# Row maxima and softmax sums that change layout by DMA, biases that leave TensorE or fill its rows, and a new order of the steps

## The reference

```python
B, S, D = 8, 512, 128
xn = layernorm(x)                                  # no affine part
out = x + attn(xn, W_qkv, W_out) + ffn(xn, ...)
# attn: 16 heads of 64, rotary embedding on q and k, causal softmax(q k / 8) v, times W_out
# ffn:  q, k, v = xn W + b; 16 heads of 8; full softmax(q k / sqrt(8)) v; a = that Wo + bo
#       x2 = xn + layernorm(a, g1, be1); gate = softmax(x2 Wg + bg); best 2 of 8 experts
#       m = sum over the 2 of gate * (x2 We[e] + bexp[e]);  ffn = x2 + layernorm(m, g2, be2)
```

## Time and profile before

| what | value |
|---|---|
| time, median of 3 runs | 1494.18 us (1490.78 to 1495.87) |
| the profiled execution | 1491.08 us, its span 1489.3 us |
| granted clock of PE, mean | 0.939 of full |
| PE busy | 1366.0 us, 92% |
| DVE, POOL, ACT busy | 920.0, 826.8, 797.6 us |
| HBM traffic | 5.59 MB read, 2.10 MB written |

### The profile page before, as it was taken

One profiled execution on the slowest core, in us unless ns is written; L12 is line 12 of the kernel. 1 busy time (PEld: TensorE's weight loads), 2 busy tenths in 40 slices (PEclk: granted clock), 3 DMA queues, 4 the chain that ended last, 5 costly groups with the idle time before them and its releaser, 6 DMA issues.

```text
span 1489.3 us, 27676 instructions
## 1 busy us (share of the span) xinstructions
PE 1366.0 (92%) x9896; PEld 842.6 (57%) x9896; DVE 920.0 (62%) x2324; ACT 797.6 (54%) x1103; POOL 826.8 (56%) x797
## 2 busy tenths in 40 slices
PE   0779999989999999989999899997999899999986
PEld 0455556646665566645576455654666555764544
DVE  5437547855567746775478655785458664786624
ACT  1256564566545664555644656454655566446550
POOL 0745557466656558355573666655564655826621
PEclk9779998999889998999989999899999999899997
DMA  3201111010101111011110111001010111101000
GB/s 108 50 8 24 28 33 33 22 36 23 29 23 29 32 28 36 8 36 30 29 30 22 36 30 29 23 22 36 23 39 13 36 30 29 30 17 34 23 1 7
DMA packets 37516, 43.04 MB, mean 29 GB/s; under 512 B 9342, under 2 KB 20870, under 8 KB 37256
## 3 DMA queue, kind: packets, MB, share of 16 engines
q1 hardware_dynamic: 34200, 38.33, 10.8%
q10 hardware_dynamic: 3184, 2.95, 0.7%
HBM read 5.59 MB, written 2.10 MB: 5 GB/s over the span
## 4 chain that ended last, share of the span: by engine, by line
PE 71%; POOL 9%; DMA 5%; ACT 4%; DVE 4%; issue 3%; SPq 2%; ACTq 0%; POOLq 0%; DVEq 0%
PE work L925 9%; PE work L833 8%; PE work L950 8%; PE work L834 5%; PE work L835 5%; PE work L837 5%; PE work L1008 4%; PE work L939 4%; PE work L971 4%; DMA swapped<-raw 3%; PE work L980 3%; PE work L901 3%; SPq L399 2%; PE work L997 2%; POOL raw L437 2%
## 5 line engine op out<-in xcount | busy, mean ns | idle before, releaser
L696 DVE TENSOR_REDUCE fnmax<-work 128x2 f32<-128x1024 f32 x256 | 301.4, 1218 | 102.8 <-PE work L980 102.5
L518 ACT ACTIVATE fpt<-work 128x1024 f32<-128x1024 f32 x256 | 250.1, 1024 | 117.3 <-PE work L997 116.1
L437 POOL TENSOR_TENSOR raw<-raw,cos_t 128x512 f32<-128x512 f32 x128 | 164.1, 1282 | 247.3 <-DMA swapped<-raw 246.6
L794 DVE CUSTOM_DVE_ANT_0 work<-work,causal 128x512 f32<-128x512 f32 (+3 forms) x512 | 235.5, 522 | 69.0 <-PE work L901 69.0
L454 POOL TENSOR_SCALAR_AFFINE_SELECT pt<-pt 128x256 f32<-128x256 f32 x128 | 49.7, 410 | 296.0 <-ACT pt L566 296.0
L566 ACT ACTIVATE pt<-work 128x1024 f32<-128x1024 f32 (+1 forms) x192 | 163.4, 882 | 93.4 <-PE work L925 89.1
L446 POOL TENSOR_TENSOR qk_l<-raw,qk_h 128x512 fp32r<-128x512 f32 x128 | 162.2, 1278 | 22.3 <-ACT qk_h L548 22.3
L441 POOL TENSOR_TENSOR raw<-raw,swapped 128x512 f32<-128x512 f32 x128 | 163.8, 1279 | 10.0
L438 POOL TENSOR_TENSOR swapped<-swapped,sin_t 128x512 f32<-128x512 f32 x128 | 164.1, 1282 | 0.0
L950 PE MATMUL work<-pt,v 128*64 128x512 f32 (+3 forms) x1024 | 158.3, 453 | 0.0
L1008 PE MATMUL work<-fpt,fv 128*9 128x512 f32 x1024 | 123.4, 593 | 0.8 <-DVE u L811 0.8
(11 more groups left out here) (167 smaller groups left out, 2688.5 us busy)
## 6 DMA issues: line engine op xcount, KB each, us to landing
swapped<-raw SPq DMA_DIRECT2D x512, 64.0 KB, 2.0
x_in<-in_L_attn_x_dram SPq DMA_DIRECT2D x8, 256.0 KB, 3.0
out_dram<-x_in SPq DMA_DIRECT2D x8, 256.0 KB, 2.3
fpt<-in_L_attn_W_qkv_dram ACTq DMA_DIRECT2D x1, 1536.0 KB, 6.8
pt<-in_L_ffn_We_dram ACTq DMA_DIRECT2D x1, 512.0 KB, 9.9
wout<-in_L_attn_W_out_dram ACTq DMA_DIRECT2D x1, 512.0 KB, 10.0
pt<-in_rope_dram ACTq DMA_DIRECT2D x1, 192.0 KB, 7.9
affine<-in_L_ffn_g_dram SPq DMA_DIRECT2D x2, 64.0 KB
```

Of the source, the lines that this page charges most:

```text
L437: nc.gpsimd.tensor_tensor(raw[:, n % 3], raw[:, n % 3], cos_t[:], ALU.mult)
L518: nc.scalar.activation(fpt[:, i, 2 * r:2 * r + 2].rearrange("p h n -> p (h n)"), bank_of(("fst", b, g, i), 2 * r, 2), ACT.Exp, scale=1.0 / ...
L696: nc.vector.tensor_reduce(fnmax[:, j, 2 * r:2 * r + 2, 0:1], bank_of(("fsm", b, g, j), 2 * r, 2).rearrange("p (f n) -> p f n", f=2), AX.X, ...
L794: ins = nc.vector.tensor_tensor_reduce(out=scores, in0=scores, in1=causal[:, S - n:S], scale=-1.0, scalar=3.0e38, op0=ALU.add, op1=ALU.min ...
```

## The change

It does five things.

1. **Row maxima.** `nmax` becomes 128 x 8 without gaps, and one transpose gives 8 rows of 128. `row` copies them to `m_rows`, and a new SP step `mrow` puts them by four DMAs of two rows into rows 0 and 64 of `max_row`, which is zero elsewhere. `st` waits for `mrow`. In the full attention `fnmax` becomes 128 x 16, `fsub` is a copy of 16 rows to `fm_rows`, and a new SP step `fput` writes them by four DMAs into rows 0, 32, 64, 96 of `fqk`; `fst` waits for it.
2. **Softmax sums.** `lT`, `fan`, `rT`, `rb` go. SP steps take their place: `lc` spreads each of four rows of `l_rows` over 128 partitions x 4, `inv` works on that, `lr` writes each inverse back as one row, `lw` copies each row to 64 partitions of `l_wide`. `lw` waits on SP until `lr` has landed; `div` waits for `lw`.
3. **Biases.** Those of `moe`, `fv`, `wo` become passes of 128 rows: `pick_row` (ones in rows 0 and 64) by `biases` (bias in row 0, its rest in row 64). Those of `fqk` go from PE: `fqkh` becomes two ACT operations with scale and bias, and `fqkl` adds a bias per partition. That of `gate` is added by DVE in `gsub`.
4. **Start.** 24 small DMAs load `qk_bias`, one `bg_rows`.
5. **Order.** All numbers of `START`, `PSUM` and `PERIOD` (170.28 to 158.1397) are new.

The core of the diff:

```diff
-    "mT": [16.58, 25.78, 57.5, 78.17, 108.69, 121.66, 144.89, 165.47],
+    "mT": [17.141, 61.043, 75.721, 95.372, 108.783, 128.409, 142.363, 154.925],
-PERIOD = 170.28
+PERIOD = 158.1397
-    "SP": ("swap", "store", "load"),
+    "SP": ("swap", "mrow", "lc", "lr", "lw", "fput", "store", "load"),
+PARTS = {"mrow": T, "lc": 4, "lr": 2, "lw": 2, "fput": T}
...
+                elif kind == "mrow":
+                    c = x_[2]
+                    sp.wait_ge(*after("row", b, c))
+                    sp.wait_ge(*after("st", *ring(1, b, c, NC), 2))
+                    for t in range(T):
+                        sp.dma_start(max_row[0:P:DH, t * P:(t + 1) * P].bitcast(F32), m_rows[2 * t:2 * t + 2].bitcast(F32)).then_inc(done["mrow"], 16)
+                elif kind == "lc":
+                    c = x_[2]
+                    sp.wait_ge(*after("lsb", b, c))
+                    sp.wait_ge(*after("inv", *ring(1, b, c, NC)))
+                    for n in range(4):
+                        row = l_rows[n * STRIP:n * STRIP + 1].rearrange("o (p j) -> o p j", j=T)
+                        sp.dma_start(l_part[:, n // 2, n % 2], row).then_inc(done["lc"], 16)
+                elif kind == "lr":
+                    c = x_[2]
+                    sp.wait_ge(*after("inv", b, c))
+                    sp.wait_ge(*after("lw", *ring(1, b, c, NC)))
+                    for h in range(2):
+                        row = r_rows[h:h + 1].rearrange("o (p j) -> o p j", j=T)
+                        sp.dma_start(row, l_inv[:, h]).then_inc(done["lr"], 16)
+                elif kind == "lw":
+                    c = x_[2]
+                    sp.wait_ge(*after("lr", b, c))
+                    sp.wait_ge(*after("div", *ring(1, b, c, NC)))
+                    for h in range(2):
+                        sp.dma_start(l_wide[h * DH:(h + 1) * DH], r_rows[h:h + 1].unsqueeze(1).broadcast_to([1, DH, S])).then_inc(done["lw"], 16)
+                elif kind == "fput":
+                    g = x_[2]
+                    sp.wait_ge(*after("fsub", b, g))
+                    for t in range(T):
+                        sp.dma_start(fqk[0:P:STRIP, g % 2, 0, t * P:(t + 1) * P].bitcast(F32), fm_rows[t * GH:(t + 1) * GH].bitcast(F32))\
+                            .then_inc(done["fput"], 16)
...
-                    nc.scalar.copy(fqk[:, g % 2].rearrange("p k n -> p (k n)"), bank_of(("fqk", b, g), 0, 2)).then_inc(done["fqkh"], 1)
+                    for k, low in enumerate((q_low, k_low)):
+                        ins = nc.scalar.activation(fqk[:, g % 2, k], bank_of(("fqk", b, g), k), ACT.Identity, scale=low,
+                                                   bias=qk_less[:, k, g:g + 1])
...
-                            out=fqk[:, g % 2, k], in0=fqk[:, g % 2, k].bitcast(F32), scalar=low, in1=bank_of(("fqk", b, g), k),
-                            op0=ALU.mult, op1=ALU.add)
+                            out=fqk[:, g % 2, k], in0=bank_of(("fqk", b, g), k), scalar=qk_bias[:, k, g:g + 1],
+                            in1=fqk[:, g % 2, k].bitcast(F32), op0=ALU.add, op1=ALU.add)
...
-                    nc.vector.tensor_tensor(fqk[:, g % 2, 0], bank_of(("fmT", b, g)), fqk[:, g % 2, 0].bitcast(F32),
-                                            ALU.add).then_inc(done["fsub"], 1)
+                    nc.vector.tensor_copy(fm_rows, bank_of(("fmT", b, g))[0:T * GH, 0:P]).then_inc(done["fsub"], 1)
...
-                                     (one_rows("bv"), bias_rows("bv")))
+                                     (pick_row[:], bias_of("bv")))
...
-                    for t in range(T):
-                        ins = nc.tensor.transpose(psum[:, tile(t)], nmax[:, t:t + P], ident)
-                    ins.then_inc(done["mT"], 1)
+                    nc.tensor.transpose(psum[0:2 * T, 0:P], nmax[:].rearrange("p t h -> p (t h)"), ident).then_inc(done["mT"], 1)
```

More of the change, by code:

```diff
@@ L51 @@
 START = {
[L52 to L67, removed]
@@ L96 @@
[L96 to L108, removed]
@@ new lines @@
+    "fT": [135.67, 161.633, 194.364, 220.297],
+    "fdiv": [143.344, 175.071, 192.304, 216.292],
+    "cT": [222.856],
+    "ch": [225.402],
+    "cl": [218.06],
+    "wo": [225.483],
+    "ln1": [224.091],
+    "rs1": [219.833],
+    "nm1": [235.204],
+    "x2": [251.609],
+    "x2T": [242.267],
+    "x2h": [257.623],
+    "x2l": [247.399],
+    "gate": [254.513],
+    "gsub": [260.49],
+    "gexp": [279.268],
+    "pick": [270.752],
+    "moe": [266.171, 267.623, 268.968, 272.316],
+    "moew": [278.221, 278.665, 278.678, 278.686],
@@ L145 @@
-    "fv": [3],
-    "fqk": [2, 1, 1, 1],
-    "fsm": [4, 2, 4, 4, 4, 0, 4, 4, 4, 4, 4, 0, 2, 4, 0, 4],
-    "fmT": [2, 0, 0, 6],
-    "fst": [2, 4, 4, 4, 4, 0, 2, 4, 4, 2, 4, 4, 4, 2, 4, 2],
-    "fpv": [3, 0, 0, 0],
-    "fT": [0, 0, 0, 0],
-    "cT": [0],
-    "wo": [2],
-    "x2T": [1],
-    "gate": [6],
-    "moe": [0, 2, 0, 2],
-    "proj": [6, 1, 6, 1, 7, 6, 0, 3, 2, 0, 5, 6, 0, 4, 0, 2],
[9 rows of a table removed]
+    "xT": [2],
+    "fv": [1],
+    "fqk": [4, 0, 6, 5],
+    "fsm": [2, 2, 4, 4, 4, 2, 0, 0, 3, 3, 4, 0, 4, 4, 4, 4],
@@ L167 @@
+    "fmT": [3, 0, 2, 2],
+    "fst": [0, 1, 3, 1, 1, 4, 0, 1, 2, 0, 2, 0, 3, 0, 0, 2],
+    "fpv": [5, 1, 7, 6],
+    "fT": [7, 3, 7, 3],
+    "cT": [2],
+    "wo": [0],
+    "x2T": [0],
+    "gate": [4],
+    "moe": [4, 2, 6, 0],
+    "proj": [6, 2, 0, 1, 2, 2, 4, 7, 2, 3, 0, 7, 0, 4, 2, 7],
[7 rows of a table added]
 }
-PERIOD = 170.28
+PERIOD = 158.1397
 ENGINE = {
     "PE": ("xT", "fv", "fqk", "fsm", "fmT", "fst", "fpv", "fT", "cT", "wo", "x2T", "gate", "moe", "proj", "v", "sm", "mT",
-           "st", "ls", "pv", "lT", "rT", "ao"),
-    "ACT": ("xh", "fvc", "fqkh", "fexp", "fo", "ch", "x2h", "gexp", "raw", "hi", "vc", "row", "exp", "lsb", "fan", "rb"),
+           "st", "ls", "pv", "ao"),
+    "ACT": ("xh", "fvc", "fqkh", "fexp", "fo", "ch", "x2h", "gexp", "raw", "hi", "vc", "row", "exp", "lsb"),
@@ L191 @@
         KEYS[kind] = [(c, unit, h) for c in range(NC) for unit in range(3) for h in range(2)]
-    elif kind in ("mT", "row", "tri", "ls", "lsb", "pv", "lT", "inv", "fan", "rT", "rb", "div"):
+    elif kind in ("mT", "row", "mrow", "tri", "ls", "lsb", "lc", "lT", "inv", "fan", "rT", "rb", "lr", "lw", "pv", "div"):
         KEYS[kind] = [(c,) for c in range(NC)]
@@ L556, in _ @@
                     act.wait_ge(*after("mT", b, c))
-                    act.wait_ge(*after("st", *ring(1, b, c, NC), 2))
-                    nc.scalar.copy(max_row[:], bank_of(("mT", b, c))).then_inc(done["row"], 1)
+                    act.wait_ge(*after("mrow", *ring(1, b, c, NC)))
+                    nc.scalar.copy(m_rows, bank_of(("mT", b, c))[0:2 * T, 0:P]).then_inc(done["row"], 1)
                 elif kind == "exp":
```

304 lines of the change are left out of this document (141 added, 163 removed), and 22 rows, old and new, of tables (PSUM, START).

## The result

The changed kernel takes **2094.63 us** (median of 4 runs, 2092.39 to 2100.75) beside 1492.48 us for the kernel before on the same chip (4 runs, 1480.22 to 1495.87). The ratio is 1.406, 95% interval 1.398 to 1.415: slower by 602 us, where 1405 us and a gain were forecast. The range, 1340 to 1465 us, does not hold it. The profiled execution took 2092.39 us, its span is 2090.7 us, and its granted clock was 0.80 after 0.939.

What follows compares the result with a forecast made beforehand. PE was taken to bound the kernel at 166.3 us per batch. Taking off 24.7 and giving back 14 saves 10.7 over seven batches; with -12 for fill and drain and +1 for start, 1491.1 becomes 1405 us, range 1340 to 1465.

Steps and rivals of the forecast that it cites:

- What bounds the kernel, and what PE loses: PE bounds the steady stage at 166.3 us per batch; fewer bias passes and transposes take 24.7 us per batch off it.
- A microsecond removed from PE is a microsecond gained, until waits take its place: In every batch, less PE work shortens the time one for one until waits replace it; PE alone would allow 141.6 us.
- Landing of `lw`: Copy of each inverse row to `l_wide`: a landing of 2.0 us, 2.6 us for the step with two issues.
- The chain of sums: Softmax sums to `div` through `lsb`, `lc`, `inv`, `lr`, `lw`: 10.2 us instead of about 3.4, costed at nothing on PE.
- Give-back of the row maxima: Waits before `st` and `fst` for `mrow` and `fput` give back 14 us per batch, bounds 5 and 22.
- Start: 25 more small DMA issues put the last load 7 us later; +1 us taken in all.
- Fill and drain: Both ends, bound by one batch's chain: less other PE work between steps but longer hops; -12 us, bounds 0 and -25.
- SP becomes the bound: Rival: small SBUF copies issue so slowly (1.3 us) that SP sets a 186 us period, 1630 us in all; chance 0.07.
- In-order DVE: Rival: `inv` and `div` wait for landings and hold up `fmax` and `max` behind them; 56 us more, 1461 us; chance 0.09.
- Clock: Rival: PE's granted clock falls around eight waits per batch, costing 50 us in all, 1455 us; chance 0.08.
- Bias passes keep their gap: Rival: full-height bias passes of `moe`, `wo`, `fv` gain nothing, 4.9 us per batch less, 1444 us; chance 0.03.
- too low: Signs that the give-back was underestimated: granted clock below 0.9, or DVE's waits for `l_part` and `l_wide` ending ahead of PE waits.

Runs made afterwards that it cites:

- e5: The changed kernel without `lr` and `lw`, `u` multiplied by a row of cosines, output not normalised: 1495.3 us, ratio 1.003 to the kernel before.
- g1: e5 with the row maxima as before the change (four transposes, no `mrow` or `fput`), output not normalised: 1420.76 us, ratio 0.954.
- f1: The kernel before, in its own order, with the change's biases alone: 1451.0 us, ratio 0.975.
- f6: f1 with `lc` taking the softmax sums from row to column by DMA in place of `lT`: 1457.1 us, ratio 0.981.
- e1: The changed kernel with each `lw` reading 64 partitions of a constant table instead of one row 64 times, output not normalised: 1645.22 us, ratio 1.104.
- e2: The changed kernel with `lw` copying an eighth of the columns, still from one partition, most output not normalised: 1645.84 us, ratio 1.104.
- e3: The changed kernel with `lw` kept, but `div` waiting for `inv` instead of it, output not normalised: 1789.95 us, ratio 1.201.
- g4: The changed kernel with `div` placed later in DVE's list in seven of eight head pairs: 2121.47 us, ratio 1.426.
- g6: e4 with `div` placed later in DVE's list, as in g4: 1715.22 us, ratio 1.153.
- f4: All mechanisms of the change, with the slow `lw`, in the order of the kernel before: 1910.66 us, ratio 1.284.
- g5: e1 with `div` placed later in DVE's list, as in g4, output not normalised: 1697.94 us, ratio 1.141.
- e4: The changed kernel with the inverses written to a DRAM row by `lr` and read from there by `lw`, whole computation: 1668.11 us, ratio 1.118.
- h1: The kernel before with the change's biases and row maxima, in the old order, the DMAs of `mrow` issued by ACT: 1591.39 us, ratio 1.071.

## Why the prediction was wrong

By its own steps:

- **What bounds the kernel, and what PE loses: right for the work, not for what it is worth.** Matmuls fell to 9000 as forecast. The sum of 24.7 us a batch is 198 us over eight; e5 shows 140 less busy time at a somewhat lower clock, g1 144 where its terms sum to 155, f1 76 where they sum to 90. In the change itself it is 57. The full-height bias pass steps by 0.23 us, as taken. The timeline of PE in the last `moe` shows it and the clock at once:

```profile
2066.30 0.63 PE L862 MATMUL work<-we_l,ct_h 128*128 128x512 f32 x1
2066.73 0.63 PE L864 MATMUL work<-biases,pick_row 128*128 128x512 f32 x1
...
2069.24 0.39 PE L862 MATMUL work<-we_l,ct_h 128*128 128x512 f32 x1
2069.47 0.39 PE L864 MATMUL work<-biases,pick_row 128*128 128x512 f32 x1
```

  At first the same 512 columns step by 0.43 us, further on by 0.23. The granted clock is 0.50 from 2065.3 to 2068.4 us and 1.00 from 2068.8 to 2072, so first 1.2 and then 2.4 GHz, with PE busy throughout both; ahead of them, from 2056 to 2065.2, it was busy for 3.8 of 9.2 us, at 0.50. The rule of the Trainium skill (TensorE: Matmul & The Clock Gate, Part 3, "What overlaps and what doesn't"), by which a full-height load would leave a gap, is not borne out as that section has it: the step with the bias is that of the passes beside it.
- **"A microsecond removed from PE is a microsecond gained, until waits take its place": half right.** Of the 90 us taken from PE in f1, 37 came off the time; of a further 31 in f6, with its slower `rb`, none did.
- **Landing of `lw`, taken as 2.0 us from the rows of `swap`: wrong, 7.0 us for the first and 10.7 for the second of a pair.** With the issues the step was put at 2.6 us and took 11.2. A `swap` reads 32 partitions, `lw` one. The row was chosen for its queue and its memory, and how wide its source is was not asked; the rule on ports that the Trainium skill has, above, was not weighed. This one number is worth 449 us: e1 and e2 against the change. At least 145 of it fall on others' transfers and issues (e3 against e1), which the forecast did not have at all; 305 us are the wait (change against e3). But it is not all: with the landing as short as forecast, e1 still takes 1645 us, 180 above the range.
- **The chain of sums "costed at nothing on PE; its cover is that distance" from `ls` to `pv`: wrong in kind.** A cover of "5 to 20 us" is short of a chain of 10.2 by the forecast's own numbers, and the term was put at nothing all the same. The chain took over 18.9 us in the stretch shown. The 3.4 us given for the chain of before are its steps without their waits: from the start of `lsb` to the end of `rb` the trace has 12.6 us at least and 17.9 in the median, which that order covered. But the distance that counts lies behind `pv`, from it to the next user of its bank and to `ao`, and there either order has but two or three steps. With short landings the last two hops still cost 150 us (e1 against e5). g4 to g6 show that a later place of `div` on DVE does not cure it. That the bank and not `u` is the reason at `fst` is read from the tables and the counts; no run gave those steps another bank (`fst` takes four, and the `fsm` just ahead of it holds the other four). In the old order this is not the mechanism: PE waits for `u` 27 us in f4, and the slow landing costs 255 us all the same.
- **Give-back of the row maxima, 14 us a batch: near in size by luck, wrong in place.** g1 gives 75 us net, and 117 gross or 14.6 a batch only if the forecast's own 42 us are added. PE's waits at `st` and `fst` for the new DMAs, which were to be the 14 us, are 19 us in the whole of e5; the rest has another cause. In the old order the hops cost twice as much net, 151 us.
- **Start: nothing where +1 us was forecast** (first transpose at 33.9 us against 34.3). **Fill and drain, taken as -12 us, within 0 and -25: wrong, +87 us.** They are one batch's chain, as the forecast says, and the long hops lie in it; with the last two hops gone (e5) span less seven batches is 302 us, 23 under the kernel before, so the term was right for short hops.
- **SP's issues** had medians of 0.49 to 0.60 us, near the 0.63 taken with gaps.
- **The rivals.** *SP becomes the bound* had the sign, not the mechanism: no issue has a median near 1.12 us, and SP waits 456 us for `raw` alone. *In-order DVE* named the right wait, `u` behind `l_wide`, at 56 us; that its mechanism is the price is not shown: g4 takes a third of that wait away, g5 two thirds, and both are slower. *Clock* was no alternative but an addition: the same 9000 matmuls are busy for 1226.0 us in e5 at 0.92 and for 1308.8 in the change at 0.80, 83 us more, which go with the lower clock. *Bias passes keep their gap* did not occur. The forecast had added its cases apart, while the runs with the longer waits are those with the lower clock (0.94 in f1, 0.89 in e1, 0.80 in the change).
- Of its signs, two spoke as it said for "too low", a clock under 0.9 and DVE waiting for `l_wide`; and PE's share in the steady stage is 65%, not about 90.

Open: how the 150 us of the short hops divide between latency and SP's queue, where most of the 75 us of the maxima lies, and why f1 keeps less than half of PE's gain. The new order with neither kind of hop was not run, so what the order alone is worth is open too.

## What to carry to other kernels

Before a copy is costed by a row of the trace, compare how many partitions each of its sides has: one row of SBUF read 64 times landed four times later than 64 rows read once, and it held up other transfers. When a hop with latency enters a chain, look for its cover behind it too, at the next user of the PSUM bank that the chain's last step frees, and count PE's steps up to that. Of a change with several parts, the one that only takes work off the busiest engine (here the biases, 1451 us) can be kept, and one run apart would have told it.

## What the runs showed of the hardware beyond that

- A DMA that reads one SBUF partition at this length delays others: issues of `swap` rose from 2.0 to 4.8 us at the longest, landings of `swap` from 4.0 to 10.0 us; with 64 source partitions (e1) they stay at 1.8 and 3.8 us.
- Through DRAM the same spreading of a row landed in 2.9 us after a write of 1.6 us, so a detour was faster than the direct way: 3.5 us for the pair instead of 11.2 (e4, 1668 us).
- DMAs issued by ACT took a median of 0.48 us each, as those of `mrow` on SP (h1).
